# FP4 feed-forward around an attention: VectorE's order, two passes on ScalarE, and the scales of a pair split together

## The reference

```python
def fp4_quant_dequant(x):      # blocks of 16 along the last dim
    xb = x.reshape(shape[:-1] + (shape[-1] // 16, 16))
    scale = jnp.maximum(jnp.max(jnp.abs(xb), -1, keepdims=True) / 6.0, 1e-12)
    idx = jnp.searchsorted(_MID, jnp.abs(xb / scale))
    return (_GRID[idx] * jnp.sign(xb / scale) * scale).reshape(shape)
def ffn(x):                    # w_gate, w_up (704, 256), w_down (256, 704)
    gate, y = fp4_linear(x, w_gate), fp4_linear(x, w_up)
    return fp4_linear(jax.nn.silu(gate) * y, w_down)   # fp4_linear quantizes both operands
x = x + 0.5 * ffn(layernorm(x))
x = x + causal_attention(layernorm(x), Wq, Wk, Wv)
x = x + 0.5 * ffn(layernorm(x))
```

## Time and profile before

| | us |
|---|---|
| median of 3 runs (1304.34 to 1307.16) | 1306.92 |
| the profiled execution's own time | 1305.54 |
| its span, first to last instruction | 1303.7 |
| busy: TensorE, VectorE, ScalarE, GpSimd | 1171.6, 1049.9, 731.8, 581.7 |

### The profile page before, as it was taken

The page is one execution under the profiler, slowest core; times in us unless marked ns, Lnnn a source line. Parts: engine busy times, 40 slices in busy tenths (PEclk is TensorE's granted clock), DMA queues, the critical chain, the costliest instruction groups (busy, mean ns, idle before and its releaser), DMA issues.

```text
span 1303.7 us, 25393 instructions
## 1 busy us (share of the span) xinstructions
PE 1171.6 (90%) x7673; PEld 743.8 (57%) x7673; DVE 1049.9 (81%) x3445; ACT 731.8 (56%) x1475; POOL 581.7 (45%) x531
## 2 busy tenths in 40 slices
PE   2689999999998689989998999999999999999997
PEld 1256555555555456666676667556665555555554
DVE  7899999999999666547545654664899999999997
ACT  4656666766764345435533543565666766666653
POOL 2444544554454245435443453454454454454442
PEclk9899999999999899999999999999999999999999
DMA  6944444344444447645663665555255454544545
GB/s 221 228 94 83 80 80 90 71 88 82 76 86 77 90 93 118 102 111 93 110 126 78 115 100 110 102 97 113 51 105 106 100 110 96 109 101 98 112 102 121
DMA packets 462750, 134.46 MB, mean 103 GB/s; under 512 B 441297, under 2 KB 461905, under 8 KB 462673
## 3 DMA queue, kind: packets, MB, share of 16 engines
q1 hardware_dynamic: 454928, 125.62, 49.9%
q10 hardware_dynamic: 7744, 7.86, 1.9%
HBM read 11.34 MB, written 8.39 MB: 15 GB/s over the span
## 4 chain that ended last, share of the span: by engine, by line
DVE 32%; PE 29%; issue 22%; ACT 6%; POOL 5%; DMA 2%; SPq 1%; DVEq 1%; ACTq 0%; POOLq 0%
PE ps L1495 12%; PE ps L1483 10%; DVE arena L940 5%; DVE arena L1000 5%; DVE arena L944 3%; POOL arena L540 3%; POOL arena L529 2%; PE ps L1468 2%; PE ps L1461 2%; DVE arena L929 2%; PE ps L1448 2%; ACT arena L669 2%; DVE arena L889 2%; ACT arena L708 2%; DVE arena L953 2%
## 5 line engine op out<-in xcount | busy, mean ns | idle before, releaser
L1448 PE MATMUL ps<-wguT,arena 128*128 128x512 f16 (+1 forms) x2304 | 480.2, 363 | 6.6 <-DMA arena<-arena 6.4
L1448 PEld LDWEIGHTS ps<-wguT,arena 128*128 128x128 f16 x2304 | 226.0, 98 | 227.9 <-issue 10.4
L540 POOL TENSOR_TENSOR arena<-arena 128x704 f32<-128x704 f32 x128 | 192.2, 1501 | 336.3 <-DVE arena L953 336.2
L1409 PE MATMUL ps<-wdT,arena 128*128 128x256 f16 x2176 | 262.7, 275 | 67.9 <-DMA arena<-arena 65.4
L1409 PEld LDWEIGHTS ps<-wdT,arena 128*128 128x128 f16 x2176 | 205.5, 98 | 131.6 <-issue 77.9
L567 POOL TENSOR_TENSOR arena<-arena 128x128 f16<-128x128 f32 (+7 forms) x64 | 143.8, 2248 | 238.2 <-ACT arena L769 198.8
L715 ACT ACTIVATE arena<-arena 128x704 int16<-128x704 f32 x128 | 100.7, 787 | 199.2 <-POOL arena L540 199.2
L1495 PE MATMUL ps<-arena 128*128 128x256 f16 x1632 | 191.0, 275 | 10.7 <-DVE x_sb L1122 10.6
L778 ACT ACTIVATE arena<-ps,arena,cst 128x128 f16<-128x128 f32 (+7 forms) x64 | 80.4, 1257 | 198.0 <-DVE arena L1111 191.5
L1483 PE MATMUL ps<-arena 128*128 128x512 f16 (+3 forms) x960 | 187.5, 348 | 2.6 <-ACT arena L769 2.6
L1495 PEld LDWEIGHTS ps<-arena 128*128 128x128 f16 x1632 | 159.3, 98 | 38.4 <-issue 8.0
(11 more groups left out here) (127 smaller groups left out, 1445.8 us busy)
## 6 DMA issues: line engine op xcount, KB each, us to landing
out_dram<-x_sb SPq DMA_DIRECT2D x32, 256.0 KB, 2.7
x_sb<-in_L_attn_x_dram ACTq DMA_DIRECT2D x3, 2048.0 KB, 9.1
arena<-arena SPq DMA_TRANSPOSE x384, 3.5
arena<-arena SPq DMA_DIRECT2D x8, 256.0 KB, 3.0
arena<-arena SPq DMA_DIRECT2D x4, 512.0 KB, 3.6
x_sb<-in_L_attn_x_dram ACTq DMA_DIRECT2D x1, 1536.0 KB, 7.3
arena<-in_L_ffn_w_down_dram SPq DMA_DIRECT2D x1, 704.0 KB, 8.4
arena<-in_L_ffn_w_gate_dram SPq DMA_DIRECT2D x1, 640.0 KB, 4.5
```

What stands on the lines that cost most here:

```text
L540: g.tensor_tensor(hy[u].rearrange("p (j b) -> p b j", j=BL), h[u].rearrange("p (b j) -> p b j", j=BL), hri[u].unsqueeze(2).to_broadcast([P ...
L1409: i = nc.tensor.matmul(ps_dn[w % 2], hT[w][:, c * P:(c + 1) * P], wdT[:, k, :], start=(s == 0), stop=(s == len(DOWN_STEPS) - 1))
L1448: i = nc.tensor.matmul(psf[:, 1536 * u + lo:1536 * u + hi], xv[:, u, xl, kt, :], wguT[:, wl, lo // P:hi // P, kt, :], start=(s == 0), stop ...
```

## The change

Three things are changed. The factor h_fc and x's code pass x_c go from VectorE to ScalarE. The joint steps of the scales (h_max, h_pow, h_inv, h_sp, h_sd, h_sh, h_sl, h_fc) are done once for the pair on double width (88 scales), in single buffers (h_fc in two). VectorE's order within the pair is another, and its loop has four pairs in the body (6 times), with 2 unrolled before it and 6 behind; the loops of the other engines stay at two pairs.

```diff
+        def act_h_fc(gp, odd):
+            nc.scalar.wait_ge(h_pw, gp + 1)
+            nc.scalar.activation(hfc[odd], hpw, ACT.Identity, scale=cst[:, C_D:C_D + 1]).then_inc(h_fc, 1)
+        def act_x_c(q):
+            nc.scalar.wait_ge(x_n, q + 1)
+            nc.scalar.wait_ge(x_q, q)
+            nc.scalar.activation(xc, xn, ACT.Copy, scale=0.25 * CODE, bias=0.125 * CODE).then_inc(x_c, 1)
...
                 if late:
                     act_h_c(n - 1, 1 - u)
+                    if u == 0:
+                        act_h_fc(gp - 1, 1 - odd)
+                if u == 0 and x2:
+                    act_x_c(gp + 2)
                 if u == 0 and x4:
                     act_x_mean(gp + 4, p + 4, odd)
...
+        def dve_h_max(gp):
+            V.wait_ge(h_s, 2 * gp + 2)
+            V.tensor_reduce(hmx, of_two(hs2), axis=AX.X, op=ALU.max).then_inc(h_mx, 1)
+        def dve_h_sp(gp):
+            V.wait_ge(h_in, gp + 1)
+            V.tensor_tensor(of_two(hsp), of_two(hs2), hin.unsqueeze(2).to_broadcast([P, 2, HB]), ALU.mult
+                            ).then_inc(h_sp, 1)
...
+        def dve_pair(gp, qd, p, odd, start=None, x2=True, x3=True, end=False, adds=False):
+            a, k = 2 * gp, None if start is None else 2 * start
+            down = k is None or k >= 4
+            dve_h_rin(a, 0)
+            if down:
+                dve_res(gp - 2, odd, 0, p * 2 - 4)
+            if adds:
+                dve_last_add(TB - 2)
+            dve_h(a + 1, 1)
+            dve_h_amax(a + 1, 1)
+            if x2:
+                dve_x_sh(gp + 2)
+            if k != 0:
+                dve_h_q(gp - 1, 1, quad(qd, 2 * odd - 3))
+            if x2:
+                dve_x_sl(gp + 2)
+                dve_x_g(gp + 2)
+            dve_h_s(a + 1, 1)
+            if x2:
+                dve_x_q(gp + 2, 0, (qd + odd, 1 - odd))
+            dve_h_g(a, 0)
+            if x2:
+                dve_x_q(gp + 2, 1)
+
+            dve_h_rin(a + 1, 1)
+            if x3:
+                dve_x_amax(gp + 3)
+            dve_h_max(gp)
+            if x3:
+                dve_x_s(gp + 3)
+            if down:
+                dve_res(gp - 2, odd, 1, p * 2 - 3)
+            if adds:
+                dve_last_add(TB - 1)
+            if x3:
+                dve_x_rin(gp + 3)
+            dve_h_pow(gp)
+            if not end:
+                dve_h(a + 2, 0)
+                dve_h_amax(a + 2, 0)
+            dve_h_inv(gp)
+            if x3:
+                dve_x_sd(gp + 3)
+            dve_h_sp(gp)
+            if not end:
+                dve_h_g(a + 1, 1)
+            dve_h_sd(gp)
+            if not end:
+                dve_h_s(a + 2, 0)
+            dve_h_sh(gp)
+            dve_h_sl(gp)
+            dve_h_q(gp, 0, quad(qd, 2 * odd - 2))
...
-                with dve.Fori(0, (NP - 6) // 2) as i:
-                    dve_pair(i * 2 + (first + 2), i + (first // 2 + 1), i * 2 + 2, 0)
-                    dve_pair(i * 2 + (first + 3), i + (first // 2 + 1), i * 2 + 3, 1)
+                with dve.Fori(0, (NP - 8) // 4) as i:
+                    for j in range(4):
+                        dve_pair(i * 4 + (first + 2 + j), i * 2 + (first // 2 + 1 + j // 2), i * 4 + (2 + j), j % 2)
```

More of the change, by code:

```diff
@@ L154, in macaron_block_kernel @@
         hq = [carve(2 * F, f16) for _ in range(2)]
[L155 to L165, removed]
+        ham2, hs2, hri2, hsp, hsd = (carve(2 * HB) for _ in range(5))
+        ham, hs, hri = ([v[:, u * HB:(u + 1) * HB] for u in range(2)] for v in (ham2, hs2, hri2))
+        hsp2 = carve(4 * HB, f16)
+        hsh, hsl = hsp2[:, 0:2 * HB], hsp2[:, 2 * HB:4 * HB]
+        hmx, hpw, hin = (carve(2) for _ in range(3))
+        hfc = [carve(2) for _ in range(2)]
         assert at[0] <= pT_late
@@ L879, in _ @@
                 act_h_c(n - 1, 1)
+                act_h_fc(first + NP - 1, 1)
                 if not first:
@@ L953, in dve_h_rin @@
             V.reciprocal(hri[u], hs[u]).then_inc(h_rin, 1)
[L955 to L983, removed]
@@ L985, in dve_h_sl, with of_two, dve_h_pow @@
-        def dve_h_sl(n, u):
-            V.wait_ge(h_sh, n + 1)
-            V.tensor_tensor(hsl[u], hsp[u], hsh[u], ALU.subtract).then_inc(h_sl, 1)
+        def of_two(v):
+            return v.rearrange("p (u b) -> p u b", u=2)
+        def dve_h_max(gp):
+            V.wait_ge(h_s, 2 * gp + 2)
+            V.tensor_reduce(hmx, of_two(hs2), axis=AX.X, op=ALU.max).then_inc(h_mx, 1)
+        def dve_h_pow(gp):
+            V.wait_ge(h_mx, gp + 1)
+            V.tensor_scalar(hpw.bitcast(i32), hmx.bitcast(i32), EXP_BITS, None, ALU.bitwise_and).then_inc(h_pw, 1)
@@ new lines, in dve_h_inv, with dve_h_sd @@
+        def dve_h_inv(gp):
+            V.wait_ge(h_pw, gp + 1)
+            V.tensor_scalar(hin.bitcast(i32), hpw.bitcast(i32), -1, H_INV_BITS, ALU.mult, ALU.add).then_inc(h_in, 1)
+        def dve_h_sp(gp):
+            V.wait_ge(h_in, gp + 1)
+            V.tensor_tensor(of_two(hsp), of_two(hs2), hin.unsqueeze(2).to_broadcast([P, 2, HB]), ALU.mult
+                            ).then_inc(h_sp, 1)
+        def dve_h_sd(gp):
+            V.wait_ge(h_sp, gp + 1)
+            V.scalar_tensor_tensor(hsd, hsp, SPLIT9, hsp, ALU.mult, ALU.subtract).then_inc(h_sd, 1)
@@ L989, in dve_h_g, with dve_h_sh, dve_h_sl @@
+        def dve_h_sh(gp):
+            V.wait_ge(h_sd, gp + 1)
+            V.scalar_tensor_tensor(hsh, hsp, SPLIT9, hsd, ALU.mult, ALU.subtract).then_inc(h_sh, 1)
+        def dve_h_sl(gp):
+            V.wait_ge(h_sh, gp + 1)
+            V.tensor_tensor(hsl, hsp, hsh, ALU.subtract).then_inc(h_sl, 1)
         def dve_h_g(n, u):
@@ L992, in dve_h_g, with dve_h_q @@
             V.tensor_scalar(v, v, ROUND_CODE, ROUND_CODE, ALU.add, ALU.subtract).then_inc(h_g, 1)
[L994 to L998, removed]
+        def dve_h_q(gp, u, landed):
+            V.wait_ge(h_g, gp * 2 + (u + 1))
+            V.wait_ge(h_sl, gp + 1)
+            if not isinstance(gp, int) or gp >= 1:
                 V.wait_ge(h_T[landed[1]], landed[0] * 16 + 16)
@@ L1001, in dve_h_q @@
                             hc[u].rearrange("p (j b) -> p j b", j=BL).unsqueeze(1).to_broadcast([P, 2, BL, HB]),
[L1002 to L1008, removed]
+                            hsp2.rearrange("p (l u b) -> p l u b", l=2, u=2)[:, :, u].unsqueeze(2
+                            ).to_broadcast([P, 2, BL, HB]), ALU.mult).then_inc(h_q, 1)
@@ L1009, in dve_res @@
+        def dve_res(gp, odd, u, tile):
+            V.wait_ge(d_mm, 2 * gp + u + 1)
+            V.wait_ge(h_fc, gp + 1)
             xs_ = x_sb[:, bass.ds(tile * D, D)]
-            V.scalar_tensor_tensor(xs_, ps_dn[w % 2], hfc[w], xs_, ALU.mult, ALU.add).then_inc(res, 1)
+            V.scalar_tensor_tensor(xs_, ps_dn[u], hfc[odd][:, u:u + 1], xs_, ALU.mult, ALU.add).then_inc(res, 1)
         def dve_last_add(i):
             dve_attention_add((B - 1) * TB + i, i, ((B - 1) * TB + i) * D)
[L1016 to L1063, removed]
@@ L1367, in _ @@
                 dve_h_amax(2 * first, 0)
+                dve_h_s(2 * first, 0)
                 if not first:
@@ L1373, in _ @@
                     wv_planes()
-                dve_pair(first + 1, first // 2, 1, 1, start=1, adds=((TB - 2, 0), (TB - 1, 1)) if first else ())
+                dve_pair(first + 1, first // 2, 1, 1, start=1, adds=(first > 0))
                 if not first:
                     m_planes()
-                with dve.Fori(0, (NP - 6) // 2) as i:
-                    dve_pair(i * 2 + (first + 2), i + (first // 2 + 1), i * 2 + 2, 0)
-                    dve_pair(i * 2 + (first + 3), i + (first // 2 + 1), i * 2 + 3, 1)
-                for k in range(NP - 4, NP):
+                with dve.Fori(0, (NP - 8) // 4) as i:
+                    for j in range(4):
+                        dve_pair(i * 4 + (first + 2 + j), i * 2 + (first // 2 + 1 + j // 2), i * 4 + (2 + j), j % 2)
+                for k in range(NP - 6, NP):
                     if not first and k == NP - 4:
@@ L1390, in _ @@
                 n = 2 * (first + NP)
-                dve_res(n - 4, 0, NT - 4)
+                dve_res(first + NP - 2, 0, 0, NT - 4)
                 dve_h_g(n - 1, 1)
-                dve_h_q(n - 1, 1, (n // 4 - 1, 1))
+                dve_h_q(first + NP - 1, 1, (n // 4 - 1, 1))
                 for j in range(3, 0, -1):
-                    dve_res(n - j, -j % 4, NT - j)
+                    dve_res(first + NP - (j + 1) // 2, j <= 2, j % 2, NT - j)
                     if not first:
```

## The result

The changed kernel takes 1333.24 us (median of 4 runs, 1328.58 to 1335.11); the kernel before, beside it, 1306.16 (4 runs). The ratio is 1.0201, interval 1.0184 to 1.0218: slower by 2.0%. The forecast was 1344, slower: 37 us more than before, where 27 were measured.

A forecast was written before the change was run, and what follows sets the result against it. VectorE was taken as the bound before; in the new order four stretches with waits make a pair 12.71 us against 12.06. 56 x 0.65 = 36.4, plus 1 for the ends, gave 1344 us; own range 1329 to 1358.

The forecast's parts named there:

- S3: Stretch of VectorE's pair from odd inverse to odd rounding h_g, with x_s held by GpSimd's h_y: 5.35 us.
- T: Time of one pair in the feed-forward loop, sum of four stretches: 12.63, with the loop's return 12.71, against 12.06 us.
- Rival (B): x_s is not held inside GpSimd's h_y: S3 4.54, T 11.90, 1299 to 1306 us; chance 10%.
- S1: Stretch from even inverse to even rounding h_g, through GpSimd and ScalarE: 4.76 us, VectorE waiting some 0.65.
- S2: Stretch of VectorE's pair from even rounding h_g to odd inverse: 0.59 us.
- S4: Stretch from odd rounding h_g to the next even inverse (rounding, split steps, scale, product): 1.93 us.
- The ends: First two and last four pairs of each feed-forward pass: between 3 us better and 5 worse, taken as +1.
- Part 1: Work leaving VectorE: 1.3 to 1.5 us a pair, some added back, leaving 10.6 us of work for VectorE.
- Rival (A): Neither chain comes late, VectorE does 10.6 and TensorE bounds at 11.17 us a pair: 1257 us; chance 6%.
- Part 3: ScalarE's added code pass and factor, ahead of the odd SiLU: covered by some 0.5 us, costed at 0.
- Part 5: VectorE's loop of four pairs: return stalls 0.3 us, like the old loop, not the attention's 4.1; 0.08 a pair.
- rival (C): The four-pair loop's return costs what the attention's does: 39 us on the forecast, 1383 us; chance 6%.

The follow-up runs named there:

- Experiment 1: Changed kernel with x's maximum and scale x_s moved from behind the odd tile's inverse to just before the even rounding h_g: 1302.09 us.
- experiment 3: Changed kernel with VectorE's loop back at two pairs in the body: 1329.08 us, ratio 1.0170 to the kernel before.
- experiment 9: Changed kernel with the orders of VectorE, GpSimd and ScalarE all rewritten: 1281.74 us, ratio 0.9816 to the kernel before.
- experiment 4: Changed kernel with x's code pass back on VectorE, behind x's first split step: 1332.62 us, ratio 1.0198 to the kernel before.
- experiment 5: Kernel before the change with only x's code pass moved to ScalarE, ahead of x's means: 1319.41 us, ratio 1.0108.
- experiment 6: Kernel before the change with only VectorE's loop made one of four pairs: 1303.82 us, ratio 0.9979.
- experiment 10: Changed kernel with VectorE's order alone rewritten, GpSimd and ScalarE keeping theirs: 1305.97 us, ratio 0.9998 to the kernel before.
- experiment 7: The kernel with the early x scale (Experiment 1), its two-element joint power h_pow written as two one-element operations: 1301.93 us.
- experiment 2: Changed kernel with x's scale x_s and inverse x_rin moved behind the next tile's h: 1373.0 us, ratio 1.0495 to the kernel before.

## Why the prediction was right

**S3, x_s held inside h_y: right, and shown.** Forecast 1.04 after the odd inverse, held to 2.04, the residual at 1.95, x's inverse at 2.33, the rounding at 5.35. Read above: 1.03, to 2.03, 1.84, 2.24, 5.19. Experiment 1 removes it: T falls by 0.53, 30 us over 56 pairs, and 31 were measured. Rival (B) is out, since x_s was held in every pair. That its T of 11.90 is near experiment 1's 11.93 is in part chance: in two neighbouring pairs there S1 is 4.89 and 5.01, where (B) had 4.76, and S3 4.32 and 4.40, where it had 4.54.

**S1, the even chain's wait: right, and 0.05 too long.** Forecast 4.76 with a wait of 0.65; measured 4.71 with 0.55. VectorE's own work in the stretch was as counted.

**S2 0.59 and S4 1.93: measured 0.59 and 1.97.** 4.71 + 0.59 + 5.19 + 1.97 = 12.46.

**The sizes that were off.** Three small terms were too slow, and S4 was 0.04 too fast. The way back from ScalarE's end to VectorE's start was taken as 0.10; it is 0.03 and 0.04 in the changed kernel (207.04 to 207.07, 212.81 to 212.85). The operation behind a held one starts 0.19 before its end, not 0.09. The loop's return was taken as 0.08 a pair and is 0: it falls into a wait that is there anyway, and experiment 3 doubles the returns and T stays. (Where that wait is gone a return does cost: in experiment 1 the pair behind one takes 12.1 in the first pass where the others of the loop take 11.84 to 11.90.) All in all 0.25: T grew by 0.40, not 0.65, 22.4 us over 56 pairs instead of 36.4.

**The ends.** Forecast +1. The spans differ by 27.7, so 5.3 us lie outside the 56 pairs: from the first h to the last the first pass grew by 14.2 (of which 11.2 are its 28 pairs) and the second by 11.7, the attention by 0.6 and the tail by 1.1. The distances of the products h say which pairs pay. The very first pair of each pass is 1.65 longer, because its even rounding waits 1.40 and 1.03 for the code pass where the kernel before waited for nothing there: the forecast had named this and priced it too low; the second is 1.2 longer in the first pass and 0.6 shorter in the second; the last three of a pass are together 1.0 and 0.7 longer. The estimate was mis-sized by 4, to the fast side, while T was mis-sized by 14 us to the slow side. That the two partly cancel is luck: with its T alone put right the forecast would have been 1330, with its ends alone put right 1348.

**Part 1, VectorE's work of 10.6.** The forecast's own terms do not give this number: 12.06 less 0.16 and less 1.3 to 1.5, with the 0.25, 0.1 and 0.1 that it adds and the 0.07 that the loop saves, is 10.8 to 11.0; in 10.6 the additions are left out. In the pair read above, 12.46 less the waits (1.01) and less what the hold took is 10.7. The hold took 0.72: VectorE's next operation starts 0.81 after x_s, and 0.09 after it in experiment 1. The slip costs the forecast nothing, because this work was never the bound and T is a sum of the four stretches. Rival (A) is out by the two waits; whether the 11.17 of TensorE can be reached no run shows, the best one has 11.65.

In experiment 9, in another order, VectorE's work comes to 11.4 (11.65 less 0.25). Most of the 0.7 more stands where an operation reads what the one before it wrote: from x's maximum to x_s 0.71 in place of 0.54, from x_s to x_rin 0.22 in place of 0.09, from a rounding h_g to what follows 0.37 in place of 0.26, from h_inv to what follows 0.20 in place of 0.07. The rest was not separated.

**Part 3, the cover of ScalarE.** Costing x's code pass at 0 was right for this change (experiment 4: the same either way) and would have been wrong by 13 us for the edit by itself (experiment 5). **Part 5** was right in that nothing like the attention's 4.1 us comes; rival (C) is out, and the loop alone gains some 2 us (experiment 6). The stall at the return did not stay 0.3, as the forecast said: it is 0.18.

**Where the saved work went.** Before, 12.06 held 11.75 of work, 0.16 of waiting for the SiLU and 0.15 of stall at the return. VectorE lost 1.0 of the work and the pair grew by 0.40: two waits for the code pass (1.01) and the held scale (0.72) took its place and that of the old waits. The waits were created by placing each rounding right behind the inverse that starts its chain. VectorE's order alone (experiment 10) only moves them to h; with GpSimd's and ScalarE's orders changed too (experiment 9) 0.25 a pair is left.

## What to carry to other kernels

When work is taken off the busiest engine, first measure the chain through the others from the operation that feeds it to the one that waits for it, and count how much of the busy engine's work stands between the two in the new order; if it is less than the chain, the saving turns into a wait. A short VectorE operation that feeds such a chain must not be placed where a long GpSimd one runs, if it is of a form that is held (below). An order is a property of all the engines together: VectorE's last order by itself only came level with the kernel before, and with the two others' it is 1.8% faster.

## What the runs showed of the hardware that was not expected

- A tensor_scalar of one element a partition is not held by GpSimd's h_y (0.10 and 0.15 us inside it in all 25 pairs of experiment 7, 0.14 or 0.15 in the kernel before). One of two elements is held until h_y ends: 0.93 in experiment 1, 0.60 in experiment 2, about 0.36 in experiment 10, where it takes 0.10 outside. So is one of 32 elements (1.00), and a scalar_tensor_tensor of 32 with two tensors in on-chip memory (0.91).
- VectorE's h, with an operand in the matmul's output memory, and the reciprocal run inside h_y at their usual length (203.36, 0.94; 203.03, 0.34).
- A held operation's successor starts up to 0.2 us before h_y's end (209.50 against 209.65, 203.50 against 203.68). The held one's record can last much longer than that, to the end of the next GpSimd operation (1.89 in 14 of 25 pairs of experiment 1), without the successor starting later.
- The hold works the other way too: a GpSimd operation of two elements that starts with VectorE's product h_q takes 0.94 instead of 0.20, in every pair between 100 and 400 us of the kernel before, and its record ends 0.04 to 0.06 after the product's.
- The stall at a loop's return depends on the order around it: 0.31 us in the kernel before, 0.18 in the changed one, at another operation. What it costs depends on the wait behind it: nothing there, 0.2 us for the pair in experiment 1.
